# A two-FFN hybrid model: the second FFN matmul's first quarter moved into the normalise-and-transpose stage, evictions moved to VectorE

## What is computed

```
x = x + attn_a(layernorm(x), ...)
x = x + ffn(layernorm(x), w_fc, w_proj)
x = x + attn_b(layernorm(x), ...)
x = x + ffn(layernorm(x), w_fc, w_proj)

def bitlinear(x, w):                       # ffn = bitlinear(gelu(bitlinear(x, w_fc)), w_proj)
    xn = layer_norm(x)
    gamma = max(abs(xn), axis=-1)
    x_hat = clip(xn * 128 / gamma, -128 + 1e-6, 128 - 1e-6) * gamma / 128
    w_hat = sign(round(w / (mean(abs(w)) + 1e-6))) * mean(abs(w))
    return x_hat @ w_hat.T                 # w_fc: 8192 x 2048, w_proj: 2048 x 8192
```

## Time and profile before

| | us |
|---|---|
| median of 2 runs (35408.72 and 35726.79) | 35567.75 |
| the profiled execution's own time | 35519.55 |
| its span on the slowest core, core 1 | 35518.0 |
| spans of all cores | 35269.3 to 35518.0 |
| busy over the span: PE, DVE, ACT, POOL | 51%, 48%, 19%, 14% |
| DMA, mean over the span | 65 GB/s |

### The profile page before, as it was taken

How to read it: one execution, slowest core, us unless ns; L and a number is a source line. 1 busy time by engine, 2 the same in 40 slices (tenths; PEclk the granted TensorE clock), 3 DMA queues, 4 the chain that set the end, 5 groups by cost and what they waited for, 6 DMA issues and landing times.

```text
span 35518.0 us, 212731 instructions; the slowest of 8 cores (35269.3 to 35518.0 us)
## 1 busy us (share of the span) xinstructions
PE 18043.2 (51%) x69249; PEld 7123.5 (20%) x69249; DVE 16875.9 (48%) x12673; ACT 6714.4 (19%) x5635; POOL 5090.0 (14%) x2020
## 2 busy tenths in 40 slices
PE   3412189318944756666633355433333437961599
PEld 1101034213422222122200011100000113421234
DVE  2246500461010018888888877788888431026200
ACT  1100211230012124422222211222221021123100
POOL 0001000000000003333332222222333100000000
PEclk7655589658966977777755566555555667875688
DMA  1155222223352110000000011000000122222232
GB/s 59 65 184 161 95 87 90 82 83 118 125 182 85 49 49 26 28 26 28 25 10 9 8 48 52 19 9 8 9 9 9 64 79 77 73 88 81 102 109 90
DMA packets 416178, 2306.37 MB, mean 65 GB/s; under 512 B 67985, under 2 KB 72114, under 8 KB 298738
## 3 DMA queue, kind: packets, MB, share of 16 engines
q1 hardware_dynamic: 260978, 1613.21, 13.6%
q0 software_dynamic: 154112, 679.54, 5.2%
HBM read 1613.10 MB, written 679.48 MB: 65 GB/s over the span
## 4 chain that ended last, share of the span: by engine, by line
DVE 43%; PE 34%; ACT 7%; DMA 6%; issue 6%; DVEq 2%; POOLq 1%; another core or an unknown queue 1%; ACTq 1%; SPq 0%; PEldq 0%; POOL 0%
DVE b_hbuf L1478 16%; DVE b_mbuf L1503 7%; DVE b_bbuf L1467 7%; PE f2d_ps L1191 6%; PE f2b_ps L1063 6%; PE f1b_ps L1063 5%; PE f1d_ps L1191 5%; PE b_psI L1616 4%; PE b_ps L1703 2%; DMA b_ys<-sp_y 1%; DVEq L191 1%; PE b_psb L1404 1%; DMA sp_inpT<-pb_ts 1%; DVE pf_sgn L914 1%; DVE f2c_st L1118 1%
## 5 line engine op out<-in xcount | busy, mean ns | idle before, releaser
L1478 DVE TENSOR_TENSOR_SCAN b_hbuf<-b_abuf,b_bbuf 128x2048 f32<-128x2048 f32 x1024 | 5721.3, 5587 | 263.1 <-DVEq L191 262.7
L1515 POOL TENSOR_TENSOR b_ybuf<-b_ybuf,b_mbuf 128x2048 f32<-128x2048 f32 x960 | 4316.1, 4496 | 9741.9 <-DVEq L191 9741.9
L1492 PE MATMUL b_psc<-b_crows,mc 128*128 128x512 bf16 x4096 | 1965.2, 527 | 6573.4 <-DVEq L191 6573.4
L1616 PE MATMUL b_psI<-b_lnT,b_w 128*128 128x512 bf16 x10240 | 2999.4, 459 | 500.6 <-DMA b_w<-sp_inpT 287.7
L1444 ACT ACTIVATE b_abuf<-b_dtT,b_Ab 128x2048 f32<-128x2048 f32 x1024 | 2051.5, 2003 | 6354.2 <-DVEq L191 6318.6
L1503 DVE TENSOR_TENSOR b_mbuf<-b_hbuf,b_psc 128x512 f32<-128x512 f32 x3840 | 2638.1, 687 | 876.2 <-issue 803.0
L1467 DVE TENSOR_TENSOR b_bbuf<-b_dtx,b_psb 128x1024 bf16<-128x1024 bf16 x2048 | 2501.3, 1221 | 559.7 <-DVEq L191 240.6
L1191 PE MATMUL f2d_ps<-f2d_w,f2d_h 128*128 128x512 bf16 x8192 | 2117.9, 431 | 122.9 <-DMA f2d_h<-sp_hhT 122.9
L1063 PE MATMUL f2b_ps<-f2b_wq,f2b_xs 128*128 128x512 bf16 x8192 | 2007.8, 415 | 117.9 <-DMA f2b_xs<-sp_xhT 117.9
L1492 PEld LDWEIGHTS b_psc<-b_crows,mc 128*128 128x128 bf16 x4096 | 376.0, 104 | 8315.4 <-issue 8226.5
L1453 PE MATMUL b_psb<-b_brows,mb 32*128 32x512 bf16 x4096 | 1822.0, 592 | 415.7 <-DVEq L191 415.7
(11 more groups left out here) (259 smaller groups left out, 16439.5 us busy)
## 6 DMA issues: line engine op xcount, KB each, us to landing
pf_wl<-L_ffn_w_fc SPq DMA_DIRECT2D x128, 1024.0 KB, 6.5
pf_wl<-L_ffn_w_proj SPq DMA_DIRECT2D x128, 1024.0 KB, 6.2
f1d_h<-sp_hhT SPq DMA_DIRECT2D x64, 2048.0 KB, 9.0
f2d_h<-sp_hhT SPq DMA_DIRECT2D x64, 2048.0 KB, 9.9
pb_wl<-L_attn_b_in_proj_w SPq DMA_DIRECT2D x80, 1024.0 KB, 7.4
b_w<-sp_inpT SPq DMA_DIRECT2D x160, 512.0 KB, 3.3
f1b_xs<-sp_xhT SPq DMA_DIRECT2D x128, 512.0 KB, 3.3
sp_h<-f1b_h POOLq DMA_DIRECT2D x128, 512.0 KB, 2.9
```

Of the source, the lines that this page charges most:

```text
L1478: return nc.vector.tensor_tensor_scan(out=hbuf[:, :], data0=abuf[asl][:, :], data1=bbuf[:, :], initial=0.0, op0=ALU.mult, op1=ALU.add)
L1492: return nc.tensor.matmul(psC[cs][:, :], self.mc[:, n * 128:(n + 1) * 128], crows[:, q * 512:(q + 1) * 512], start=True, stop=True)
L1515: return nc.gpsimd.tensor_add(ybuf[:, :], ybuf[:, :], mbuf[msl][:, :])
L1616: return nc.tensor.matmul(psI[:, :], statT[:, dk * 128:(dk + 1) * 128], lnT[:, dk * L + off:dk * L + off + 512], start=(dk == 0), stop=(dk ...
```

## The change

Three edits.

1. In stage a of `ffn` and in `emit_ln` of attention b, the copies out of PSUM move from ACT to DVE, and PE waits for DVE in place of ACT.
2. Stage c and the first 512 output columns of stage d become one loop. The first weight block is loaded ahead of the first row on SP's queue. The row buffer `hrow`, its quantised copy `hhb` and the staging tile become single; the transposed tile stays in one of two `hh` buffers, from which it is stored and also used by 64 matmuls. Scale and bias are applied by ACT. The upper quarter of the two quantising operations goes to POOL, on a semaphore of its own, `sp`; transposes of groups 6 and 7 wait for it. The evictions are on DVE. A tile's residual add comes one tile late, ahead of the next tile's evictions.
3. Stage d goes over the other 1536 columns in three passes of 512, each with its own load of 8.4 MB of weights and of all 32 transposed tiles. Even tiles are loaded on SP's queue, odd ones on POOL's, where the stores of the result also are.

The core of the diff (for the stage a and `emit_ln` edits one line pair stands for each):

```diff
@@ stage a
-                    return nc.scalar.activation(
-                        out=tstage[:, g0 * 128:(g0 + 8) * 128],
-                        in_=ps_t[:, 0:1024], func=AF.Copy)
+                    return nc.vector.tensor_copy(
+                        tstage[:, g0 * 128:(g0 + 8) * 128], ps_t[:, 0:1024])
...
@@ stages c and d
+        wv = wq_load(0)
...
+        def emit_fadd(t):
...
+            p.op("vector", fadd, waits=((sm, mm_mark[sl]), xv_pair[sl]),
+                 inc=sv)
+            av[sl] = sv.n
+            xo_mark[sl] = (p.dma("gpsimd",
+                                 x_out[t * 128:(t + 1) * 128, 0:512],
+                                 xres[sl][:, :], waits=((sv, av[sl]),)),)
         for tt in range(NTT):
             sl = tt % 2
-            lv = p.dma("sync", hrow[sl][:, :],
+            lv = p.dma("sync", hrow[:, :],
                        self.sp_h[tt * 128:(tt + 1) * 128, :],
-                       waits=((sv, pv["x"][sl]),))
+                       waits=((ss, xmark_s),))
+            xv_pair[sl] = p.dma("sync", xres[sl][:, :],
+                                x_in[tt * 128:(tt + 1) * 128, 0:512],
+                                waits=((sv, av[sl]),) + xo_mark[sl])
...
-            p.op("vector", lambda sl=sl: nc.vector.tensor_scalar(
-                out=xn2h[:, :], in0=hrow[sl][:, :], scalar1=st2[sl][:, 2:3],
-                scalar2=st2[sl][:, 3:4], op0=ALU.mult, op1=ALU.add),
-                waits=((sv, rdy),), inc=sv)
+            p.op("scalar", lambda sl=sl: nc.scalar.activation(
+                out=xn2h[:, :], in_=hrow[:, :], func=AF.Identity,
+                scale=st2[sl][:, 2:3], bias=st2[sl][:, 3:4]),
+                waits=((sv, rdy), (spm, pmax_p)), inc=ss)
+            xmark_s = ss.n
...
+            p.op("gpsimd", lambda sl=sl: nc.gpsimd.tensor_scalar(
+                out=xn2h[:, HF:], in0=xn2h[:, HF:],
+                scalar1=st2[sl][:, 6:7], scalar2=self.qb[:, 0:1],
+                op0=ALU.mult, op1=ALU.min),
+                waits=((sv, stv_), (ss, xmark_s)))
+            p.op("gpsimd", lambda sl=sl: nc.gpsimd.tensor_scalar(
+                out=hhb[:, HF:], in0=xn2h[:, HF:],
+                scalar1=self.qb[:, 1:2], scalar2=st2[sl][:, 5:6],
+                op0=ALU.max, op1=ALU.mult),
+                waits=((sm, tr_last),), inc=spm)
...
+            p.op("vector", lambda sl=sl: nc.vector.tensor_scalar(
+                out=xn2h[:, 0:HF], in0=xn2h[:, 0:HF],
...
+            if tt > 0:
+                emit_fadd(tt - 1)
             for g0 in range(0, 64, 8):
+                gate = (sv, qvv) if g0 < 48 else (spm, pmax_p)
...
+                def fe(g0=g0, sl=sl):
+                    return nc.vector.tensor_copy(
+                        hh[sl][:, g0 * 128:(g0 + 8) * 128], ps_t[:, 0:1024])
+                p.op("vector", fe, waits=((sm, mmv),) + tuple(stq[sl]),
+                     inc=sv)
+                p.op("tensor", lambda: None, waits=((sv, sv.n),))
...
+            for fk in range(64):
+                def fm(fk=fk, sl=sl):
+                    return nc.tensor.matmul(
+                        psq[sl][:, :], hh[sl][:, fk * 128:(fk + 1) * 128],
+                        wqd[:, fk * 512:(fk + 1) * 512],
+                        start=(fk == 0), stop=(fk == 63))
...
-        for nch in range(2):
...
+        for q in (1, 2, 3):
+            wv = wq_load(q)
             for tt in range(NTT):
-                lv = p.dma("sync", hsl[slot][:, :], self.sp_hhT[tt, :, :],
-                           waits=((sm, hv[slot]),))
+                sl = tt % 2
+                extra = (st_marks[NTT - 2 + sl],) if q == 1 else ()
+                lv = p.dma("sync" if sl == 0 else "gpsimd", hh[sl][:, :],
+                           self.sp_hhT[tt, :, :],
+                           waits=((sm, mm_mark[sl]), st_marks[tt]) + extra)
+                xv = p.dma("sync", xres[sl][:, :],
+                           x_in[tt * 128:(tt + 1) * 128,
+                                q * 512:(q + 1) * 512],
+                           waits=((sv, av[sl]),) + xo_mark[sl])
...
+                p.op("vector", fadd, waits=((sm, mm_mark[sl]), xv), inc=sv)
+                av[sl] = sv.n
+                xo_mark[sl] = (p.dma("gpsimd",
+                                     x_out[tt * 128:(tt + 1) * 128,
+                                           q * 512:(q + 1) * 512],
+                                     xres[sl][:, :],
+                                     waits=((sv, av[sl]),)),)
@@ emit_ln of attention b
-                            return nc.scalar.activation(
...
+                            return nc.vector.tensor_copy(
+                                lnT[:, (g0 + j) * L + tt * 128:
+                                    (g0 + j) * L + (tt + 1) * 128],
+                                ps_t[:, j * 128:(j + 1) * 128])
```

More of the change, by code:

```diff
@@ L1092, in ffn @@
         sb = lambda n, s, d: es.enter_context(nc.sbuf_tensor(n, s, d)).ap()
+        spm = p.sem("sp")
         ps_t = es.enter_context(
             nc.psum_tensor(f"{tag}c_pst", [128, 1024], BF16)).ap()
-        hrow = [sb(f"{tag}c_h0", [128, FF], BF16),
-                sb(f"{tag}c_h1", [128, FF], BF16)]
+        psq = [es.enter_context(
+                   nc.psum_tensor(f"{tag}d_ps{i}", [128, 512], F32)).ap()
+               for i in range(2)]
+        hrow = sb(f"{tag}c_h", [128, FF], BF16)
         xn2h = sb(f"{tag}c_xn2", [128, FF], F32)
@@ new lines, in ffn, with wq_load @@
+        HF = (FF // 4) * 3
+        def wq_load(q):
+            nch, off = divmod(q, 2)
+            return p.dma("sync",
+                         wqd[:, :].rearrange("p (a b) -> p a b", a=64),
+                         self.sp_pjsT[nch, :, :,
+                                      off * 512:(off + 1) * 512],
+                         waits=((sm, p.sem("sm").n),))
+        wv = wq_load(0)
+        st_marks = [None] * NTT
+        stq = [((sv, 0),), ((sv, 0),)]
+        mm_mark = [0, 0]
+        ev_mark = [0, 0]
@@ new lines, in ffn, with fadd @@
+        av = [0, 0]
+        xv_pair = [None, None]
+        xo_mark = [((sv, 0),), ((sv, 0),)]
+        pmax_p = 0
+        pq_sl = [0, 0]
+        xmark_s = 0
+        tr_last = 0
+        def emit_fadd(t):
+            sl = t % 2
+            def fadd(sl=sl):
+                return nc.vector.scalar_tensor_tensor(
+                    out=xres[sl][:, :], in0=psq[sl][:, :],
+                    scalar=self.gam[:, 1:2], in1=xres[sl][:, :],
+                    op0=ALU.mult, op1=ALU.add)
+            p.op("vector", fadd, waits=((sm, mm_mark[sl]), xv_pair[sl]),
[4 more added lines that the diff above has]
+                                 xres[sl][:, :], waits=((sv, av[sl]),)),)
@@ L1129, in ffn @@
+            p.op("gpsimd", lambda sl=sl: nc.gpsimd.tensor_scalar(
[3 more added lines that the diff above has]
+                waits=((sm, tr_last),), inc=spm)
+            pmax_p = spm.n
+            pq_sl[sl] = pmax_p
             p.op("vector", lambda sl=sl: nc.vector.tensor_scalar(
[L1130 to L1131 removed]
@@ L1202, in ffn, with fm @@
-                hv[slot] = sm.n
-                mmv = sm.n
-                def fadd(slot=slot, psc=psc):
+                    def fm(fk=fk, sl=sl):
+                        return nc.tensor.matmul(
+                            psq[sl][:, :],
+                            hh[sl][:, fk * 128:(fk + 1) * 128],
+                            wqd[:, fk * 512:(fk + 1) * 512],
+                            start=(fk == 0), stop=(fk == 63))
+                    p.op("tensor", fm,
+                         waits=(wv, lv, (sv, av[sl])) if fk == 0 else (),
+                         inc=(sm if fk == 63 else None))
```

136 lines of the change are left out of this document (48 added, 88 removed).

## The result

The changed kernel takes 36630.31 us (median of 11 runs), the kernel before 35631.17 us beside it (median of 10). The ratio is 1.031 (95% interval 1.026 to 1.036): slower by 3.1%. The prediction was 36080 us with 35800 to 36450 us as its range; the time lies above the range. (Medians are over all executions; ratios and their intervals leave out the slow ones, in which one half of the chip took over 1% longer at a lower granted clock, or which lay over 1.5% above the kernel's fastest.)

The account below looks back on a forecast made before the run. Bounds: DVE's chain in c, PE in d, loads at new weight blocks. Adding +415, +78, +60 and -10 us to 35519.55 gave 36063 us for core 1; forecast 36080 us for the slowest core, range 35800 to 36450.

Parts of the forecast that it names:

- GpSimd's price: Stage c: GpSimd's quarter of scale and clip delays DVE by one operation per tile, 2.3 us; bounds 0 and 9 us.
- threshold for slower by 2%: Stage c: GpSimd cost per tile from which the kernel counts as slower, 5.4 us, total 36279 us.
- My upper bound, twice 4.5 us: Stage c: at most two full GpSimd operations per tile delay DVE, 9 us.
- The mechanism: Stage c: DVE's scale starts first, GpSimd's first operation falls in the gap before the clip and delays DVE, 2.3 us.
- The rest of the tile: Stage c: DVE's serial chain per tile without GpSimd's charge, 50.8 us, with the matmuls hidden.
- Stage d was right by its parts: Stage d: odd loads queue behind stores, stalling PE 14.5 us; pairs take 43.9 us, three passes 2221 us.
- The clock of the second FFN's d: Second FFN's d: the granted clock mostly recovers; +78 us for c and d, plus 60 us left for the rest.
- the rival of a low clock: Second FFN's d: clock stays at 0.82, pairs cost 5.3 us more, total 36270 us; chance 0.13.
- The rest of the program: Stage a and attention b's layer norm: evictions moved to DVE change 0 and gain 10 us.
- The rival of an odd load that is not slowed by its neighbour: Stage d: odd-tile stalls are 6.1 us shorter on each of 96 pairs, total 35494 us; chance 0.10.
- a double GpSimd price: Stage c: two full GpSimd operations of 4.5 us per tile delay DVE, 429 us more, total 36510 us; chance 0.14.

## Why the prediction was wrong

**The step that failed is GpSimd's price.** "The nearest is its add of the same size, 4.50 us, with two tensors in; with one in I take half, 2.3 us", and then "I charge one operation per tile, 2.3 us". The operation takes 7.23 us, more than the add from which I halved. That halving had no row behind it: nothing in the earlier trace rows says that GpSimd's time goes with the number of tensors read, and with one tensor in it came out 1.6 times the add with two. Of the 7.2 us DVE waits for 6.8, once per tile: (6.8 - 2.3) x 64 = 288 us. With the 6.8 us, the prediction's own sum gives 36370 us, and its threshold for slower by 2% (5.4 us a tile) is passed. My upper bound, twice 4.5 us, came nearest to the total by luck: it is one operation of 7, not two of 4.5.

**The mechanism was right.** DVE's scale starts first, GpSimd's first operation gets in at the gap before the clip, and DVE waits for it whole. I had read this from a scan that took 5.83 in place of 4.42 us. The Trainium skill (SBUF — State Buffer, Who interferes with whom) says the same: an exclusive hold for a whole instruction, decided by which came first. The trace agrees for operations of 1280 to 2048 columns, and disagrees for 1024, where DVE was held up for 0.7 us only. The prediction gave that rule's consequence, that the split saves nothing, in one sentence, and then charged a small price all the same; at 7 us a turn, it could only lose. The Trainium skill (GPSIMD Engine Reference, Engine selection) puts GpSimd roughly at line rate for operations with one input; here it took 7.23 us for 2048 columns, where DVE took 3.48 for 6144 and a DVE row sum over 2048 f32 columns takes 2.29 us.

**The rest of the tile**, 58.33 - 6.76 = 51.57 us against 50.8: affine 7.22 us as worked out, evictions 1.98 us apart as worked out, 0.5 us more between row sum and maximum, and 0.2 us from the one tile in 32 that GpSimd holds up twice. 0.77 x 64 = 49 us in all. The matmuls of c were hidden, as predicted: no DVE operation of the tile waits for them.

**Stage d was right by its parts.** Weight and first tile 35.9 us (36), load issued 2.3 us after the matmuls (1.8), a stall of (770.5 - 3 x 36) / 48 = 13.8 us (14.5), a pair of 8502.75 - 8458.14 = 44.6 us (43.9) with a burst of 30.07 - 13.85 = 16.2 us for the odd tile (15.5). Odd tiles waited and even ones did not. 2234 us for the three passes against 2221. These stalls, 96 x 13.8 = 1325 us, are the largest cost of the change, and they were foreseen.

**The clock of the second FFN's d** came back nearly whole in this execution: 43 us more than in the first (60 left). From c's last transpose group to the end, d took 2251 to 2294 us on all cores and in both FFNs. But the argument from the earlier trace rows doesn't carry that far. It was that in the output projection, with PE busy 71%, the bursts ran at full clock, and that d would be no denser. In the changed kernel's profile the same output projection, not touched by the change and PE busy 73%, had 0.72 on core 7, where the earlier trace rows had 0.84 on core 1:

```profile
28660.00:29370.00 710.00, 521.37 (x1829) 205.20 (x1829) 35.51 (x29) 0.00 (x0) 15.44 (x29) 0.72 0.29 98
```

Nine other profiled executions with the same stage d have it at 2237 to 2484 us, depending on the core. So that the sum met the time of d in both FFNs was in part luck. The reading behind the rival of a low clock was wrong as well ("they run this stage together as before"). The windows of the kernel before in the second FFN's d, for core 0 and core 2, show that only some cores lost the clock there:

```profile
33400.00:35200.00 1800.00, 1735.62 (x6664) 730.94 (x6799) 68.04 (x53) 0.00 (x0) 28.21 (x53) 0.82 0.30 102
...
33400.00:35200.00 1800.00, 1716.64 (x7934) 777.23 (x7935) 78.30 (x61) 0.00 (x0) 32.46 (x61) 0.98 0.36 122
```

**The rest of the program** costs 76 us more in place of 10 less, core 7 against core 1: the second thing missing, 86 us. Of it 66 us lie between the last scan's start and the next FFN's first load (844 and 779 us), most of which is the output projection above. This is a difference between two cores and no effect of the change that is shown. Averaged over all eight cores, the way from the first FFN's end to the second one's start takes 18773 us before and 18764 after, and c and d take 515 us more in the first FFN and 490 in the second.

**The profiled execution against the median.** It lies 138 us below the median of its runs, the one of before 48 us below the median that I started from. The forecast had added 17 us for that. The miss of 550 us is then 288 + 49 + 86, some 7 in d, and about 120 from this.

The rival of an odd load that is not slowed by its neighbour fell: 11.6 us from issue to landing, against 8.6 on SP beside it and 9.2 on its own queue when issued early. The rival of a low clock fell in f2's d in this execution. That of a double GpSimd price was the nearest, with 0.14.
